# Decoder layer on one core: self attention's products in high and low halves, rope tables gathered early

## The reference, cut to what matters

```python
q = (hidden_states @ Wq).reshape(b, s, 32, 16)
kv = hidden_states @ Wkv                      # one key and one value head of 16
k, v = (kv[..., :16], kv[..., 16:])
scores = jnp.einsum('bqhd,bkd->bhqk', q, k) * 0.25
bias = slopes[:, None, None] * (pos[None, None, :] - pos[None, :, None])
scores = jnp.where(causal, scores + bias, -jnp.inf)
out = jnp.einsum('bhqk,bkd->bqhd', softmax(scores), v).reshape(b, s, 512)
return out @ Wo
```

## Time and profile before

| what | before |
|---|---|
| median of 3 runs | 1014.06 us (1012.79 to 1015.66) |
| the profiled execution's own time | 1012.56 us |
| its span in the trace | 1010.7 us |
| PE busy | 983.5 us, 97% |
| DVE, ACT, POOL busy | 592.5, 429.3, 382.1 us |
| DMA, mean over the span | 40 GB/s |
| granted clock of PE, mean | 0.992 |

### The profile page before, as it was taken

The page is one execution under the profiler, slowest core; times in us unless marked ns, Lnnn a source line. Parts: engine busy times, 40 slices in busy tenths (PEclk is TensorE's granted clock), DMA queues, the critical chain, the costliest instruction groups (busy, mean ns, idle before and its releaser), DMA issues. The chain is left out here.

```text
span 1010.7 us, 15673 instructions
## 1 busy us (share of the span) xinstructions
PE 983.5 (97%) x5096; PEld 806.2 (80%) x5096; DVE 592.5 (59%) x973; ACT 429.3 (42%) x1239; POOL 382.1 (38%) x375
## 2 busy tenths in 40 slices
PE   5999999989999999999999999999999989999998
PEld 3877777777888888888888888888888768888787
DVE  3756666636776666666766657657666873343100
ACT  2777777751533533533523533433432543333100
POOL 7422222253652652642642633624523422222200
PEclk8999999979999999999999999999999999999999
DMA  6000000211120210210210210200200112222001
GB/s 203 13 11 11 11 10 10 64 53 52 44 62 1 64 42 0 73 31 0 73 31 0 73 31 0 83 20 20 74 0 1 33 32 72 64 73 65 11 32 42
DMA packets 53026, 39.98 MB, mean 40 GB/s; under 512 B 4128, under 2 KB 44192, under 8 KB 52992
## 3 DMA queue, kind: packets, MB, share of 16 engines
q1 hardware_dynamic: 52608, 38.48, 12.8%
q0 software_dynamic: 384, 1.05, 0.4%
HBM read 37.43 MB, written 2.10 MB: 39 GB/s over the span
## 5 line engine op out<-in xcount | busy, mean ns | idle before, releaser
L617 PE MATMUL bank<-cross_wo_hl,cross_outT_hl 128*128 128x512 f32 x768 | 191.7, 398 | 1.0 <-POOL cross_wo_hl L611 0.6
L617 PE MATMUL bank<-hsT_hl,cross_wqkv_hl 128*128 128x512 f32 x768 | 188.2, 394 | 0.0
L617 PEld LDWEIGHTS bank<-cross_wo_hl,cross_outT_hl 128*128 128x128 f32 x768 | 143.1, 188 | 35.5 <-POOL cross_wo_hl L611 1.6
L617 PEld LDWEIGHTS bank<-hsT_hl,cross_wqkv_hl 128*128 128x128 f32 x768 | 141.9, 188 | 29.3
L931 ACT ACTIVATE cross_scores<-cross_scores,cross_negmax 128x128 f32<-128x128 f32 x256 | 99.8, 391 | 127.1 <-DVE cross_negmax L869 127.1
L791 POOL TENSOR_TENSOR cross_qT<-rotated,rotated_other_half 128x512 f32<-128x512 f32 x64 | 82.8, 1293 | 161.9 <-DVE rotated_other_half L833 161.9
L617 PE MATMUL bank<-hsT_hl,ff_gate_upT_hl 128*128 128x512 f32 (+1 forms) x528 | 120.5, 390 | 2.7 <-DVE ff_gate_upT_hl L1133 2.7
L617 PEld LDWEIGHTS bank<-hsT_hl,ff_gate_upT_hl 128*128 128x128 f32 (+1 forms) x528 | 97.7, 185 | 25.0 <-DVE ff_gate_upT_hl L1133 3.1
L941 ACT CAST cross_outT_hl<-bank 128x512 fp32r<-128x512 f32 x64 | 37.1, 579 | 143.4 <-PE bank L617 142.5
L831 DVE TENSOR_TENSOR rotated<-bank,cosT 128x512 f32<-128x512 f32 x80 | 55.2, 690 | 71.4 <-PE bank L617 71.3
L617 PE MATMUL bank<-ctxT_hl,cross_wqkv_hl 128*128 128x512 f32 x384 | 94.3, 394 | 1.1 <-PEq L74 1.1
(11 more groups left out here) (115 smaller groups left out, 1534.1 us busy)
## 6 DMA issues: line engine op xcount, KB each, us to landing
staged_rows<-in_wq SPq DMA_DIRECT2D x32, 256.0 KB, 2.8
staged_rows<-in_wo SPq DMA_DIRECT2D x32, 256.0 KB, 2.6
staged_rows<-in_wg SPq DMA_DIRECT2D x10, 256.0 KB, 2.9
staged_rows<-in_wu SPq DMA_DIRECT2D x10, 256.0 KB, 3.0
staged_rows<-in_wd SPq DMA_DIRECT2D x10, 256.0 KB, 2.9
ctx_rows<-in_ctx SPq DMA_DIRECT2D x8, 256.0 KB, 2.8
staged_rows<-in_wk SPq DMA_DIRECT2D x8, 256.0 KB, 3.1
staged_rows<-in_wv SPq DMA_DIRECT2D x8, 256.0 KB, 3.1
```

What stands on the lines that cost most here:

```text
L617: i = nc.tensor.matmul(out, stationary[:, a], moving[:, b], start=(first and k == 0), stop=(last and k == 2))
```

## The change

It has four parts.

1. The query and output products are made from high and low halves, three float32r products in the place of one float32 product. The high half of `Wq` is taken by ACT and its low half by DVE, per quarter as it arrives, into the buffer that later holds cross attention's pieces; `Wo` is loaded behind `Wq` into the same staging rows, split by ACT (turns 1 to 4 of block 0) and POOL. The low halves of the transposed rows are new DVE operations in every block: `xnT_low` in turn 1, `attnT_low` in turn 5.
2. Keys and values come from one product (`kv_product`, eight float32r products of 64 columns) in bank `G[1]` instead of `G[0]`, behind a wait for `q_copied`. DVE adds the halves (`kv_rows`, two reductions), PE transposes the keys (`k_transpose`, turn 5), ACT and DVE split them (turn 5 instead of turn 4).
3. The rope tables are gathered on POOL between `rstd_of_x(2, SEQS)` and `body(1)`, instead of behind block 7, and are transposed and copied in block 1 turn 6, block 2 turn 6, block 7 turns 1 and 2, instead of all in block 8. The first two pieces of cross attention wait for half of that, the next for all of it.
4. The bias tables are four DVE operations of eight heads each (`bias_of`) instead of 32 on POOL.

```diff
-            pool.wait_ge(sem["rel_loaded"], 16)
-            for h in range(HEADS):
-                nc.gpsimd.tensor_scalar(bias[:, h, :], rel[:], slopes[h], None, ALU.mult).then_inc(sem["bias"], 1)
-                if h == 15:
-                    pool.wait_ge(sem["head_of_row_loaded"], 16)
-                    keys_by_head(0)
-                    rstd_of_x(1, 2)
-                    xn_of(1)
+            rstd_of_x(1, 2)
+            xn_of(1)
+            pool.wait_ge(sem["head_of_row_loaded"], 16)
+            keys_by_head(0)
+            for t in range(KT):
+                pool.wait_ge(sem["wo1_high"], t + 1)
+                nc.gpsimd.tensor_tensor(wo[:, 1, t, :], w_rows[:, t, :], wo[:, 0, t, :].bitcast(F32), ALU.subtract).then_inc(sem["wo1_low"], 1)
...
             body(0)
             rstd_of_x(2, SEQS)
+            pool.wait_ge(sem["pos_loaded"], 16)
+            pool.wait_ge(sem["wo1_low"], KT)
+            for b in range(SEQS):
+                nc.gpsimd.indirect_dma_start(
+                    tables[:, b, :], None, io["rope"], bass.IndirectOffsetOnAxis(ap=pos[:, b:b + 1].bitcast(mybir.dt.uint32), axis=0),
+                ).then_inc(sem["tables_loaded"], 16)
             body(1)
...
+            def bias_of(i):
+
+                heads = slice(8 * i, 8 * i + 8)
+                nc.vector.tensor_tensor(bias[:, heads, :], rel[:].unsqueeze(1).to_broadcast([P, 8, P]),
+                                        slope[:, heads].unsqueeze(2).to_broadcast([P, 8, P]), ALU.mult).then_inc(sem["bias"], 1)
...
                     if s < SEQS - 2 and not since(b, 1):
                         stats_of_x(s + 2)
+                    if s in (0, 1) and not since(b, 1):
+                        bias_of(s + 2)
+                    if s == 1 and front:
+                        xnT_low(b + 1)
...
                     if s == 4 and front:
                         q_low(b + 1)
-                        k_low(b + 1)
+                        kv_rows(b + 1, G[1])
+                    if s == 5 and since(b, 1):
+                        attnT_low(b)
+                    if s == 5 and front:
+                        k_low(b + 1, G[1])
...
-            def q_product(c, tiles):
+            def q_product(c, tiles, first=False):
                 for t in tiles:
-                    i = nc.tensor.matmul(G[1][:], xnT[:, t, :], wq[:, t, :], start=(t == 0), stop=(t == KT - 1))
+                    if first:
+                        pe.wait_ge(sem["wq1_low"], t + 1)
+                    for k, (a, w) in enumerate(((0, 0), (0, 1), (1, 0))):
+                        i = nc.tensor.matmul(G[1][:], xnT[:, a, t, :], wq(w, t), start=(t == 0 and k == 0), stop=(t == KT - 1 and k == 2))
...
                     if s == 4 and front:
-                        if since(b, 2):
-                            pe.wait_ge(sem["hs_low"], b - 1)
-                        kv_product(b + 1)
+                        pe.wait_ge(sem["q_copied"], b + 2)
+                        kv_product(b + 1, G[1])
```

More of the change, by code:

```diff
@@ L212, in _ @@
             body(SEQS - 1)
[L213 to L218, removed]
             for j in range(PIECES):
@@ L242, in q_low, with k_low @@
                                         ALU.subtract).then_inc(sem["q_copied"], 1)
-            def k_low(c):
+            def k_low(c, bank):
                 dve.wait_ge(sem["kv_high"], c + 1)
-                nc.vector.tensor_tensor(kT[:, 1, :], G[0][:, 0:P], kT[:, 0, :].bitcast(F32), ALU.subtract).then_inc(sem["kv_copied"], 1)
+                nc.vector.tensor_tensor(kT[:, 1, :], bank[:, P:2 * P], kT[:, 0, :].bitcast(F32), ALU.subtract).then_inc(sem["kv_copied"], 1)
+            dve.wait_ge(sem["rel_loaded"], 32)
+            bias_of(0)
+            wq_low(0)
+            xnT_low(0)
+            for t in range(1, KT):
+                wq_low(t)
+            dve.wait_ge(sem["x_second"], 16)
+            stats_of_x(1)
+            kv_rows(0, G[0])
+            k_low(0, G[0])
             q_low(0)
-            k_low(0)
             dve.wait_ge(sem["x_rest"], 16)
-            stats_of_x(1)
+            bias_of(1)
             def normalise(b, i):
@@ L360, in copy_qT, with wq_high @@
                 nc.scalar.copy(qT[:, HALF * half:HALF * (half + 1), :], G[1][:].rearrange("p (s k) -> p s k", s=HALF)).then_inc(sem["qT"], 1)
+            def wq_high(t):
+                act.wait_ge(sem[f"wq1_loaded{t}"], 16)
+                nc.scalar.copy(wq(0, t), w_rows[:, t, :]).then_inc(sem["wq1_high"], 1)
+            act.wait_ge(sem["wkv1_loaded"], 16)
+            nc.scalar.copy(wkv_hl[:, :, 0], wkv[:]).then_inc(sem["wkv1_high"], 1)
+            wq_high(0)
             copy_xnT(0, first=True)
+            for t in range(1, KT):
+                wq_high(t)
+            copy_kT(0, G[0], first=True)
             copy_q(0, first=True)
-            copy_kv(0, first=True)
             copy_qT(0, 0, first=True)
@@ L413, in body @@
                         nc.scalar.copy(block_of(ctxT[:, 0], b), ctx_rows[:]).then_inc(sem["ctx_high"], 1)
-                    if s == 5 and back and not scores:
-                        for i in range(HALF):
-                            act.wait_ge(sem["tables_transposed"], i + 1)
-                            t = ps[i][:].rearrange("p (b w k) -> p w b k", b=2, w=2)
-                            nc.scalar.copy(m["cosT"][:, 2 * i * P:2 * (i + 1) * P].rearrange("p (b k) -> p b k", b=2), t[:, 0])
-                            nc.scalar.copy(m["sinT"][:, 2 * i * P:2 * (i + 1) * P].rearrange("p (b k) -> p b k", b=2), t[:, 1])
             for b in range(3):
@@ L473, in _ @@
             xn_transposes(0)
-            pe.wait_ge(sem["xnT"], 1)
-            pe.wait_ge(sem["wq1_loaded"], 16)
-            q_product(0, range(KT))
-            pe.wait_ge(sem["wk8"], 1)
-            kv_product(0)
+            pe.wait_ge(sem["xnT_low"], 1)
+            pe.wait_ge(sem["wkv1_low"], 1)
+            kv_product(0, G[0])
+            q_product(0, range(KT), first=True)
+            k_transpose(0, G[0])
             q_transposes(0, 0)
@@ L1309, in constant_tables @@
     rope = np.concatenate([cos, cos, -sin, sin], axis=1).astype(np.float32)
-    return np.ascontiguousarray(np.concatenate([rel, own], axis=1)), rope
+    slopes = np.broadcast_to(np.array(alibi_slopes(), np.float32), (P, HEADS))
+    return np.ascontiguousarray(np.concatenate([rel, own, slopes], axis=1)), rope
 _INPUTS = {
```

154 lines of the change are left out of this document (103 added, 51 removed).

## The result

| | before | after |
|---|---|---|
| median of the runs | 1013.48 us (1012.79 to 1015.66, 4 runs) | 1057.11 us (1054.22 to 1059.07, 4 runs) |
| the profiled execution's own time, and its span | 1012.56, 1010.7 us | 1059.07, 1056.9 us |
| first product of cross attention, us from the span's start | 231.71 | 277.95 |
| mean granted clock of PE | 0.992 | 0.953 |

The ratio is 1.043 (95% interval 1.0411 to 1.0449): slower by 43.6 us where I forecast 12, and outside the range that I gave. All of it lies ahead of cross attention: 46.2 us more up to its first product, and the profiled executions are 46.5 us apart (that of the kernel after is the longest of its four).

What follows compares the result with a forecast made beforehand. PE's own work was taken to bound the repeated block before the change. Terms of +13 (start), +5.3 (blocks) and -6 (end) on 1012.56 gave 1024.9, or 1026 as median; range 1011 to 1036.

Steps and rivals of the forecast that it cites:

- Term 2: Repeated block: cheaper PE products but a new wait for `q_low`, 1.0 us longer a block, +5.3 us in all.
- Term 1: Start, blocks 0 to 1: gathers ahead of `xn_of(2)` delay PE's transposes of `xn`, +13 us.
- Term 3: End of attention: no late weight piece, no sixteen table transposes standing alone, -6 us (bounds -8.5 and -3).
- PE's work decides: Repeated blocks: PE's work, not DVE's and ACT's chain, counts; each block gives 2.3 us, total 1008; chance 0.17.
- DVE and POOL collide more: Blocks: `ctx_low` takes 2.5 instead of 1.5 us beside POOL, low halves meet in block 0: +5, 1031; chance 0.17.
- The gathers are hidden: Start: POOL's gathers cost nothing, as issue is cheaper or PE reaches block 1 later: 1013; chance 0.08.
- both rivals together: Start and blocks: PE's work sets the blocks and the gathers cost nothing: 998; chance 0.05.

Runs made afterwards that it cites:

- e5: The changed kernel with eight products that change no result in PE's pause ahead of its wait for `q_copied`: 1032.14 us, ratio 1.0179.
- e1: The changed kernel with `q_low` moved on DVE from turn 4 into turn 3, ahead of `hs_low`: 1018.34 us, ratio 1.0047.
- e4: The kernel before with one line more, PE's wait for `q_copied` ahead of `kv_product`: 1062.89 us, ratio 1.0477.
- e2: The changed kernel with the eight gathers moved on POOL behind `xn_of(2)`, ahead of `keys_by_head(2)`: 1044.44 us, ratio 1.0334.
- e7: The changed kernel with early `q_low`, late gathers, early `xnT_low`, and PE's two pauses in block 8 filled with repeated products: 1009.8 us, ratio 0.9944.
- e3: The changed kernel with both `q_low` in turn 3 and the gathers behind `xn_of(2)`: 1011.74 us, ratio 0.9988.
- e8: The changed kernel with `q_low` at the head of DVE's turn 4, ahead of bias and maximum: 1033.25 us, ratio 1.0185.
- e9: e7 with three more fillings of PE's pauses: turn 2 of block 0, twice, and ahead of block 1's first scores: 1007.77 us, ratio 0.9937.
- e11: e9 with six more filling products ahead of PE's wait for `q_copied` in block 0: 1008.08 us, ratio 0.9946.

## Why the prediction was wrong

The direction was right, and what I named happened; the size was not, as the largest cost was in none of my terms for the blocks.

**Term 2 is the step that failed.** I wrote that PE idles 1.9 us for `q_copied` and that a block becomes 26.6 us, 1.0 more than before. The pause was 2.2 us. With the clock held (e5) the block is 26.4 us. That the sum came so near is in part luck: the pause was 0.3 us longer than I had it, and `ctx_low`, which I took at 1.5 us, took 0.68 in the block of the kernel after shown above. PE's own work was counted well: six float32r products took 1.48 us to the next start, 0.74 a tile, against my 0.71, and the product of keys and values 0.92 against 0.9. What the sum lacked was the clock. The earlier trace rows showed a granted clock of 0.84 in the stretch with pauses; I priced that at the start (2 us in term 1), weighed it for the end (term 3), and left it out of every block, into each of which I was putting a new pause. It costs 30.85 - 26.41 = 4.4 us a block and 25 in all. e1 and e5 show it from both sides, and e4 shows that it needs nothing of the change but the wait. From 59.59 to block 7 the change measured +35.3 where my terms give +7.3 (term 2, and the 2 us that term 1 put behind the transposes of `xn`).

The Trainium skill (TensorE: Matmul & The Clock Gate, Part 1) says that the clock is gated by a block that watches how busy PE has lately been. The traces agree (0.80 beside pauses of 2.2 us, 1.00 beside fillings); I had not applied it to the wait that I predicted.

**Term 1** was right in kind and 4 us small: +15.2 at the transposes of `xn`, where I had 11.2 (the 13 without the 2 us behind them). I expected PE idle for some 9 us, and it was 6.2, but block 0 ran in part at half clock (0.67 from 25 to 50 us) behind its waits of 3.81 us for `xnT_low` and 1.66 for `q_low`. The keys' low half was done at 42.7, where I had 39.5 (38.6 to 41.0), and the first scores came not 2 us earlier but at 19.09 instead of 18.75. Taking the gathers out of the way gave 12.7 us (e2).

**Term 3** was -4.2 us against -6, within its bounds: the clock fell again, 5.49 us for an output product that takes 2.91 at the full one (e7). The late piece and the sixteen transposes were gone, as forecast, and from the copy of the last weight piece to cross attention were 14.2 us, just past my 10.5 to 14.

**The rivals.** "PE's work decides" did not come in the change, but e1 shows that its condition was one line away: without the pause a block is 24.1 us. Its 2.3 us a block were 1.5, since PE then waits 0.84 us for the copy of the queries (e3). "DVE and POOL collide more" did not happen in the change: `ctx_low` had 0.88 us as its median of eight and 0.68 in the block above. "The gathers are hidden" did not happen: PE stood idle for 6.24 us behind them. The 998 that I gave for both rivals together is a slip: 0 - 13 - 6 from 1014 is 995; nothing else hangs on it.

**What stays open.** Why of two pauses of 0.88 and 0.89 us only one takes the clock (e8), why pauses of the same length cost less in blocks 1 and 2 of e2, and why the clock fell in e7 where no pause was near. So the pauses are shown to be what takes the clock in nearly every block of the change, but not to be all that does. And how much of the 0.5 to 0.6% that e9 and e11 gain would remain if block 0 were ordered well instead of filled; I did not try other orders there.

## What to carry to other kernels

Where PE is the bound and a change gives it a new wait, price the wait twice: its own length, and the work behind it at half the clock, in every repetition; a pause below 1 us took the clock only in some blocks (e8), so for it this is the upper price. Look for the operation it waits for: here one subtraction stood one turn too late on DVE, and moving it was worth more than all the products that the change made cheaper. Where a pause can't be removed, harmless products in it are a test of what the clock costs, and sometimes a repair.

## What was not expected of the hardware

- One wait of 2.0 us a block, 12.2 us in all, made a kernel 49.6 us slower (e4).
- At half clock PE's busy share stays high (22.8 of 25 us at 0.80), so busy time hides the loss; instruction counts and durations of one form show it (0.96 or 1.73 us, 1.64 or 2.91).
- Eight wasted products in each of seven blocks made the kernel 25 us faster (e5).
- Removing one pause at the start raised another twice, each with its own fall of the clock (e9, e11).
- The clock fell for 3.5 us in a block in which PE had not waited for 15 us (e7).
